# A state-space scan inside a convolution, attention and expert kernel: tiles of 32 channels by 4 states instead of 8 channels by 16 states

## The reference, cut to what matters

```
# 4 directions k (rows, columns, and both reversed), D = 192 channels, N = 16 states, L = 1024 positions
x_dbl = einsum('bkdl,kcd->bkcl', xs, x_proj_weight)      # c = 6 + 16 + 16
dts, B, C = x_dbl[:, :, :6], x_dbl[:, :, 6:22], x_dbl[:, :, 22:38]
dt = softplus(einsum('bkrl,kdr->bkdl', dts, dt_projs_weight) + bias)
A  = -exp(A_logs)                                        # one value per direction, channel and state
for l in range(L):                                       # for every image, direction, channel d, state n
    h[d, n] = h[d, n] * exp(dt[d, l] * A[d, n]) + dt[d, l] * u[d, l] * B[n, l]
    y[d, l] = sum over n of h[d, n] * C[n, l]
y += Ds * u ; the four directions are summed, normalised, passed through gelu
```

## Time and profile before

| | |
|---|---|
| median of 3 runs | 3044.75 us (3038.03 to 3046.68) |
| the profiled execution | 3046.35 us, span 3044.2 us |
| DVE busy over the span | 2226.7 us (73%) |
| PE busy | 2434.6 us (80%) |
| ACT busy | 1408.0 us (46%) |
| POOL busy | 1310.4 us (43%) |
| DMA, mean over the span | 96 GB/s |

### The profile page before, as it was taken

One profiled execution on the slowest core, in us unless ns is written; L12 is line 12 of the kernel. 1 busy time (PEld: TensorE's weight loads), 2 busy tenths in 40 slices (PEclk: granted clock), 3 DMA queues, 4 the chain that ended last, 5 costly groups with the idle time before them and its releaser, 6 DMA issues. The chain is left out here.

```text
span 3044.2 us, 33683 instructions
## 1 busy us (share of the span) xinstructions
PE 2434.6 (80%) x9156; PEld 870.9 (29%) x9156; DVE 2226.7 (73%) x3030; ACT 1408.0 (46%) x1949; POOL 1310.4 (43%) x677
## 2 busy tenths in 40 slices
PE   4776767676677676767667689999999969999999
PEld 2111111111111111111113312323233216676676
DVE  4899989999999998999965588878787843221122
ACT  3344444444444454444545416767676732212221
POOL 1678877878778887778772200000000020000000
PEclk9776767777777776777767869999999969999999
DMA  3455555555555555555541431312213160000000
GB/s 90 131 166 161 157 155 155 171 157 153 158 162 150 164 171 146 158 151 159 161 114 49 105 44 23 43 24 34 34 23 43 23 144 1 11 6 6 6 6 11
DMA packets 104457, 291.18 MB, mean 96 GB/s; under 512 B 15262, under 2 KB 21057, under 8 KB 104257
## 3 DMA queue, kind: packets, MB, share of 16 engines
q1 hardware_dynamic: 103194, 289.13, 36.5%
q10 hardware_dynamic: 1102, 0.19, 0.0%
HBM read 239.66 MB, written 25.88 MB: 87 GB/s over the span
## 5 line engine op out<-in xcount | busy, mean ns | idle before, releaser
L529 POOL TENSOR_TENSOR hs<-hs,bc 128x1024 f32<-128x1024 f32 x384 | 899.9, 2355 | 218.8 <-DVE hs L615 218.6
L502 ACT ACTIVATE decay<-decay,a_neg 128x1024 f32<-128x1024 f32 x384 | 440.6, 1148 | 670.4 <-DMA decay<-dt_rows 659.3
L426 PE MATMUL psU<-stack,spread_sel 96*128 96x512 bf16 x768 | 361.4, 488 | 437.4 <-DVE hs L615 341.8
L1447 DVE TENSOR_REDUCE mx<-ps 128x1 f32<-128x512 f32 x864 | 539.5, 684 | 115.3 <-PE ps L1286 110.2
L559 DVE TENSOR_TENSOR psU<-psU,bc 128x512 f32<-128x512 f32 x768 | 517.3, 677 | 27.1 <-issue 14.9
L1422 ACT ACTIVATE P<-ps 128x512 f32<-128x512 f32 x768 | 417.7, 599 | 247.1 <-PE ps L1298 222.9
L615 DVE TENSOR_TENSOR_SCAN hs<-decay,psU 128x512 f32<-128x512 f32 x384 | 466.2, 1214 | 77.3 <-PE psY L388 49.0
L615 DVE TENSOR_TENSOR_SCAN hs<-decay,hs,psU 128x512 f32<-128x512 f32 x384 | 488.9, 1273 | 1.1
L388 PE MATMUL psY<-hs,state_sel 128*32 128x512 f32 x1572 | 398.5, 849 | 23.7 <-DVE Y L572 11.1
L1286 PE MATMUL ps<-ks,qs 96*128 96x512 bf16 x864 | 344.3, 402 | 34.5 <-DMA ks<-qk_parts 23.8
L426 PEld LDWEIGHTS psU<-stack,spread_sel 96*128 96x128 bf16 x768 | 70.8, 100 | 1005.9 <-DVE hs L615 806.4
(11 more groups left out here) (239 smaller groups left out, 2381.2 us busy)
## 6 DMA issues: line engine op xcount, KB each, us to landing
decay<-dt_rows SPq DMA_DIRECT2D x388, 512.0 KB
stack<-parts SPq DMA_DIRECT2D x297, 64.0 KB, 5.6
dt_rows<-dt SPq DMA_DIRECT2D x33, 384.0 KB, 6.9
qs<-qk_parts SPq DMA_DIRECT2D x90, 128.0 KB, 6.7
ks<-qk_parts SPq DMA_DIRECT2D x90, 128.0 KB, 7.1
qk_parts<-qparts SPq DMA_DIRECT2D x16, 576.0 KB, 3.6
X<-in_x_dram SPq DMA_DIRECT2D x4, 768.0 KB, 9.9
raw<-in_x_dram SPq DMA_DIRECT2D x4, 768.0 KB, 10.5
```

Of the source, the lines that this page charges most:

```text
L426: pe.matmul(psU[:, q % UR, :], s.spread_sel[:, gg, :], stack[:, ui % 2, j, CH * pos:CH * pos + CH], start=True, stop=True).then_inc(dtu_sp ...
L502: nc.scalar.activation(decay[:, t % DR, :], decay[:, t % DR, :], ACT.Exp, scale=s.a_neg[:, col:col + 1]).then_inc(decay_ready, 1)
L529: pool.tensor_tensor(h, h, bc[:, 2 * p + r, 1, :], ALU.mult).then_inc(hc_ready, 1)
L1447: v.reduce_max(mx[:, slot, u:u + 1], ps1[:, (slot * MAXES + u) % R, :], AX.X).then_inc(max_done, 1)
```

## The change

A tile now holds 32 channels x 4 states: partition 32*q + d is channel d, state group q, and tile t = 3*nq + j covers channels 32*j to 32*j+31 and states nq, 4+nq, 8+nq and 12+nq. What has to be spread over the partitions changes with it:

- dt comes from DRAM once for each block of 32 channels (three loads in a unit, into a ring of four `dt_rep`), and serves four tiles. ACT reads `dt_rep` and writes `decay`, which now has six buffers.
- dt*u is stored to DRAM as well and loaded in the same way (three loads, ring `dtu_rep`). DVE's product reads it.
- B is projected together with C by one narrow matmul group (64 rows, both reversals) twice in an image, split into three bf16 parts in `b_stack`, and spread by PE (`b_sel`).
- C goes to DRAM as 32 rows and is loaded four times in a unit, 4 rows each repeated 32 times (`c_rep`). POOL reads it.
- The weights' prologue copies get smaller, the A table comes in its new layout by four DMAs instead of one and a transpose, and z is prepared one unit ahead instead of two, at tiles 1 to 3.

```diff
-        HR, DR, UR = 6, 4, 4
+        HR, DR, UR, RR = 6, 6, 4, 4
-        bc = sb("bc", [128, 4, 2, L])
-        stack = sb("stack", [HC, 2, NBLK, L], BF16)
+        rows = sb("rows_bc", [3 * 2 * N, L])
+        b_stack = sb("b_stack", [3 * 2 * N, 2, L], BF16)
+        c_rep = sb("c_rep", [128, SUB, L])
+        dt_rep = sb("dt_rep", [128, RR, L])
+        dtu_rep = sb("dtu_rep", [128, RR, L])
...
+        def rep_slot(ui, j):
+            return (3 * ui + j) % RR
...
 # PE
-                        pe.wait_ge(stacked[ui % 2], in_stack(b, ui))
+                        if ui in (0, 4):
+                            pe.wait_ge(lo_ready, b * 2 + (p + 1))
...
-                                pe.matmul(psU[:, q % UR, :], s.spread_sel[:, gg, :],
-                                          stack[:, ui % 2, j, CH * pos:CH * pos + CH],
+                                pe.matmul(psU[:, q % UR, :], s.b_sel[:, r, nq, :],
+                                          b_stack[:, p, CH * pos:CH * pos + CH],
...
 # ACT
-                            act.wait_ge(landed[t % DR], n * (16 * TILES // DR) + (16 * (t // DR) + 16))
-                            nc.scalar.activation(decay[:, t % DR, :], decay[:, t % DR, :], ACT.Exp,
+                            if nq == 0:
+                                act.wait_ge(dt_in[rep_slot(ui, j)], rep_count(b, ui, j))
+                            act.wait_ge(scan_done, n * (2 * TILES) + (2 * t + 2 - 2 * DR + S0))
+                            nc.scalar.activation(decay[:, t % DR, :], dt_rep[:, rep_slot(ui, j), :], ACT.Exp,
...
 # POOL
+                            if t % NBLK == 0:
+                                pool.wait_ge(c_in[nq], n * 16 + 16)
...
-                            if t == 2:
-                                pool.wait_ge(hi_ready, n + 2)
-                                pool.tensor_tensor(rest[:], dtu[:], parts[:, 0, :], ALU.subtract).then_inc(rest_ready, 1)
-                            if t == 9:
-                                pool.wait_ge(log_ready, n + 3)
+                            if t == 3:
+                                pool.wait_ge(log_ready, n + 2)
                                 pool.tensor_tensor(dt[:], dt[:], soft[:], ALU.add).then_inc(dt_ready, 1)
...
 # DVE
+                    if t < NBLK and q % 2 == 0:
+                        v.wait_ge(dtu_in[rep_slot(ui, j)], rep_count(b, ui, j))
...
-                    v.tensor_tensor(u, u, bc[:, 2 * p + r, 0, CH * pos:CH * pos + CH], ALU.mult).then_inc(dbu_ready, 1)
+                    v.tensor_tensor(u, u, dtu_rep[:, rep_slot(ui, j), CH * pos:CH * pos + CH], ALU.mult
+                                    ).then_inc(dbu_ready, 1)
...
 # SP
-                    src = s.dt_dram[par, d:d + DD, :].unsqueeze(1).broadcast_to([DD, N, L])
-                    sp.dma_start(decay[:, t % DR, :], src).then_inc(landed[t % DR], 16)
+                def spread_rows(i, par, rep, landed, ui, j):
+                    src = s.dt_dram[par, i, BLK * j:BLK * j + BLK, :].unsqueeze(0).broadcast_to([4, BLK, L])
+                    sp.dma_start(rep[:, rep_slot(ui, j), :], src).then_inc(landed[rep_slot(ui, j)], 16)
...
+                def load_c(ui, nq):
+                    p, f, r, k = order(ui)
+                    src = s.c_dram[p].rearrange("(r q n) l -> r n q l", r=2, q=4)[r, nq]
+                    sp.dma_start(c_rep[:, nq, :], src.unsqueeze(1).broadcast_to([4, BLK, L])).then_inc(c_in[nq], 16)
...
                         sp.wait_ge(dt_ready, n + 2)
+                        store(0, par, dt, dt_stored)
...
+                        c_free(0)
+                        load_c(nu, 0)
+                        sp.wait_ge(dtu_ready, n + 2)
+                        store(1, par, soft, dtu_stored)
+                        sp.wait_ge(dt_stored, n * 16 + 32)
+                        sp.wait_ge(decay_ready, n * TILES + 1)
+                        load_dt(nu, 0)
+                        c_free(1)
+                        load_c(nu, 1)
...
+                        for j in (1, 2):
+                            sp.wait_ge(decay_ready, n * TILES + (9 + j))
+                            load_dt(nu, j)
+                        sp.wait_ge(dtu_stored, n * 16 + 32)
+                        sp.wait_ge(dbu_ready, n * (2 * TILES) + 2)
+                        load_dtu(nu, 0)
+                        sp.wait_ge(dbu_ready, n * (2 * TILES) + 20)
+                        load_dtu(nu, 1)
+                        c_free(2)
+                        load_c(nu, 2)
+                        sp.wait_ge(dbu_ready, n * (2 * TILES) + 22)
+                        load_dtu(nu, 2)
+                        c_free(3)
+                        load_c(nu, 3)
```

More of the change, by code:

```diff
@@ L256, in _ @@
                         q = 2 * k + f
[L257 to L260, removed]
+                        own(v.tensor_copy(s.w_bc[:, k % 2, f, :].rearrange("p (i r n) -> p r i n", i=2, n=N)[:, k // 2],
+                                          ps[0:HC, 1, 38 * q + R:38 * q + R + 2 * N].rearrange("p (i n) -> p i n", n=N)))
                 v.wait_ge(aexp, 1)
@@ L292, in scan @@
         psP = ctx.enter_context(nc.psum_tensor("psP", [128, 2, CH], F32))
-        landed = [sem(f"landed{i}") for i in range(DR)]
+        B_ROWS, C_ROWS, R_ROWS = slice(0, 2 * N), slice(2 * N, 4 * N), slice(4 * N, 6 * N)
+        dt_in = [sem(f"dt_in{i}") for i in range(RR)]
+        dtu_in = [sem(f"dtu_in{i}") for i in range(RR)]
+        c_in = [sem(f"c_in{i}") for i in range(SUB)]
         decay_ready = sem("decay_ready")
-        dtu_spread = sem("dtu_spread")
+        b_spread = sem("b_spread")
         dbu_ready = sem("dbu_ready")
@@ L493, in _ @@
-                for t in (9, 10, 11):
-                    z_side(t, 1, 1)
+                row_mid(0, 0)
+                z_side(3, 0, 0)
                 with act.Fori(0, NB, 1) as b:
@@ L621, in _, with store @@
             def _(sp):
-                def store(par):
-                    sp.dma_start(s.dt_dram[par], dt[:]).then_inc(dt_stored, 16)
-                def stack_up(part, slot):
-                    for j in range(NBLK):
-                        sp.dma_start(stack[BLK * part:BLK * part + BLK, slot, j, :],
-                                     parts[BLK * j:BLK * j + BLK, part, :]).then_inc(stacked[slot], 16)
-                def load(par, t):
-                    d = rows_of(t)
-                    src = s.dt_dram[par, d:d + DD, :].unsqueeze(1).broadcast_to([DD, N, L])
-                    sp.dma_start(decay[:, t % DR, :], src).then_inc(landed[t % DR], 16)
+                def store(i, par, tile, done):
+                    sp.dma_start(s.dt_dram[par, i], tile[:]).then_inc(done, 16)
@@ L635, in _, with store_c @@
+                def store_c(p):
+                    sp.dma_start(s.c_dram[p], rows[C_ROWS, :]).then_inc(c_stored, 16)
+                sp.wait_ge(row_taken, 2)
+                store_c(0)
                 sp.wait_ge(dt_ready, 1)
-                store(0)
+                store(0, 0, dt, dt_stored)
+                sp.wait_ge(dtu_ready, 1)
+                store(1, 0, soft, dtu_stored)
                 sp.wait_ge(dt_stored, 16)
-                for t in range(DR):
-                    load(0, t)
@@ L640, in _ @@
-                for part, ready in enumerate((hi_ready, mid_ready, lo_ready)):
-                    sp.wait_ge(ready, 1)
-                    stack_up(part, 0)
+                load_dt(0, 0)
+                sp.wait_ge(dtu_stored, 16)
+                load_dtu(0, 0)
+                for j in (1, 2):
+                    load_dt(0, j)
+                    load_dtu(0, j)
+                sp.wait_ge(c_stored, 16)
+                for nq in range(SUB):
+                    load_c(0, nq)
                 with sp.Fori(0, NB, 1) as b:
@@ L661, in _ @@
-                for i in range(DR):
-                    sp.wait_ge(landed[i], NB * UNITS * (16 * TILES // DR) + 16)
-                sp.wait_ge(stacked[0], (NB * UNITS // 2 + 1) * (16 * QPART * NBLK))
+                        store(0, par, dt, dt_stored)
+                        if nu in (0, 4):
+                            sp.wait_ge(c_stored, b * 32 + (32 if nu else 48))
+                            sp.sem_inc(turn_seen, 1)
+                        c_free(0)
+                        load_c(nu, 0)
@@ new lines, in _ @@
+                        load_c(nu, 2)
[3 more added lines that the diff above has]
+                        load_c(nu, 3)
+                for j in range(NBLK):
+                    slot = rep_slot(0, j)
+                    sp.wait_ge(dt_in[slot], rep_count(NB, 0, j))
+                    sp.wait_ge(dtu_in[slot], rep_count(NB, 0, j))
+                for nq in range(SUB):
+                    sp.wait_ge(c_in[nq], (NB * UNITS + 1) * 16)
```

327 lines of the change are left out of this document (166 added, 161 removed).

## The result

| | before | after |
|---|---|---|
| median | 3044.58 us (3038.03 to 3046.68, 4 runs) | 3682.16 us (3674.00 to 3684.12, 4 runs) |
| ratio | | 1.209 (95%: 1.207 to 1.212) |
| span of the profiled execution | 3044.2 us | 3681.9 us |
| DMA, mean over the span | 96 GB/s | 69 GB/s |

The changed kernel is 21% slower. It does not lose by more work: the page of after has PE, DVE, ACT and POOL all a little less busy in microseconds than before, and DVE's share has fallen from 73% to 60%.

What follows compares the result with a forecast made beforehand. It took the scan to be bound by loads on four engines: 96.9 us for the first unit, 31 periods of 82.85 and a last load put the next stage at 2774; 3046.35 + 2774 - 1558.4 gave 4260 us, range 3570 to 4530.

Steps and rivals of the forecast that it cites:

- the main case: Scan loads on four engines at the mean or low rate: 4260 us, range 3900 to 4520, chance 0.62.
- the upper rate: Rival for the scan's loads: four engines at 26.4 GB/s each, 5.0 us a load, 3604 us (3550 to 3800), chance 0.24.
- The outermost count sets the engines: Scan loads: the source's outermost count sets how many engines run, 8 before and 4 after, always the same ones.
- The rate of one engine: Scan loads: 18.3 GB/s an engine, so 7.2 us for a 512 KB load; bounds 5.0 and 8.0 us.
- The cycle of a unit: Scan: DVE and POOL work, two stores, then nine loads in a row make a period of 82.85 us, against 46.0.
- 18.05 + 9 L: Scan: a unit's period in us, 18.05 for compute and stores plus nine loads of L us each.
- τ: Scan: the moment when a unit's last load of dt*u (`dtu_rep`, j = 2) has landed.
- Start and end: Around the scan's periods: dt store at 52.8 us, next stage at 2774; A table's four small loads 0 to 12 us.
- 621 + 299 L: End of the scan: the time in us when the next stage starts, with L us for one load.
- The reading of before: Scan before the change: bound by its loads on eight engines almost as tightly as by DVE; ACT waited 659.3 us.
- Engines by distinct rows: Rival for the scan's loads: distinct source rows set the engines, only C gets four; 52 us a unit, 3240 us, chance 0.05.
- The case of more engines: Rival: loads spread over 8 to 16 engines, DVE and PE decide the scan; 2988 us, chance 0.05.

Runs made afterwards that it cites:

- the run of before on all engines: Kernel before with states outermost in a tile (partition 8*n + d), so each decay load's source is 16 copies of 8 rows: 3009.87 us, ratio 0.989.
- the kernel made for it: Changed kernel with the partition order turned over, 4*d + q instead of 32*q + d, channel outermost: 2971.12 us, ratio 0.976 to before.

## Why the prediction was right or wrong

It gave 4260 us, 3570 to 4530, slower with 0.94; the time is 3682. The direction and the mechanism were right, and one term was mis-sized, by enough that the change came out at 638 us where 1215 were forecast. The 3900 to 4520 given for the main case alone missed; 3570 to 4530 holds the result because the upper rate, a rival with a chance of 0.24, was kept in it.

- *The outermost count sets the engines.* Right. The share in loads is 0.26, and the three layouts and the split transfers agree: 4, 8 or 16 engines by that count, in the old tiles and in the new. This was seen ahead of the run in the earlier trace rows, where X with 96 rows outermost had 1.04 and `decay` with 8 had 0.51. The rule of the Trainium skill (DMA: Bandwidth & Descriptors, "Rules for kernel authors"), that a leading broadcast of c copies confines a DMA to c engines, is what after shows for c = 4, with 102 to 104 GB/s.
- *The rate of one engine.* The step that failed. The prediction took "the mean of the whole scan, 7.2 us" (18.3 GB/s an engine) for one load and gave the upper rate a chance of 0.24. Measured: 102/4 = 25.5 to 104/4 = 26.0 GB/s, 5.1 us, and 4.92 us at the end of the scan. The mean over eight engines was an average of fast and slow stretches, and its slow part doesn't carry over to four. It was carried over without a row that showed it, as the prediction says itself. Nothing in before told the two rates apart either: 62 to 66 us, with four loads queued, ran at 127 GB/s. The sign that the prediction named for this error, a share of 0.25 with 100 GB/s or more, is what the windows show.
- *The cycle of a unit.* Right. With L = 5.1 the formula 18.05 + 9 L gives 63.95 us; 65.05 were measured. The addition on POOL ends at 1023.24, 13.6 us after τ (13.4 predicted), and the store is issued at once. The share of 0.26 to the end of a burst of loads says that the waits between them were met in time. In the unit shown, of 65.5 us, 0.2 of the excess lies before the store of dt and 1.3 behind it; why was not looked into.
- *Start and end.* The first store of dt at 55.57 against 52.8 predicted, the first scan at 74.7. The next stage at 2187 us, by 621 + 299 L at 5.1 it is 2146. Of the 41 us some 34 are 31 periods that are 1.1 longer, and 3 the later store. The four small loads of the A table, allowed 0 to 12 us, cost little: with one DMA in their place, in the kernel with the channel outermost, the store is issued at 54.60, 1 us earlier.
- *The sum.* The own formula at the measured L gives 3046.35 + 2146 - 1558.4 = 3634 us, within 1.3% of 3682. The rival *four engines at their upper rate* (3604 us, 3550 to 3800) is what came.
- *The reading of before.* Right in kind, too strong in degree. "Almost as tightly as by DVE" comes to 34 us of 3044, by the run of before on all engines, and ACT's 659.3 us of waits were mostly no cost.
- *The other rivals.* Engines by distinct rows fell with the share of 0.26 in loads of 32 distinct rows. The case of more engines was worked out at 2988 us; the kernel made for it took 2971, with the wait at the place that was named.

What stays open: why eight engines move now 127 and now 211 GB/s at a standing share, and why a busy one of 16 moves now 14 and now 26. The pitch of the rows was tried and changes little if anything, and the number of rows is not it. The half loads on four engines write the same partitions of the same tiles and held 105 GB/s in the window shown, 26 an engine, so that neither the destination nor the source rows alone explain it. How many engines run at once, and with how many loads in flight, would be the next things to vary; that was not tried.

## What to carry to other kernels

When a tile repeats rows over partitions, look at the outermost count of each load's source and choose the order of the indices in a partition number so that it is 16 or a multiple (here 16, 32 and 96 used all engines). In this kernel one exchange of two indices is worth 711 us of 3682. A DMA share that stands at 4/16 or 8/16 while consumers wait is a full resource, not a free one. But idle time of a consumer that is ahead, as ACT's here, doesn't price it. For the rate that a changed resource will run at, don't carry a mean over from a stage whose stretches differ: give the time for both ends, and run the new pattern in the old kernel. The loads of before cut in two are an edit of a few lines and would have shown 105 GB/s on four engines ahead of the forecast.

## What was not expected of the hardware

The rate of a busy engine isn't one number, and it is steadiest where few engines run. Four engines stand at 102 to 105 GB/s (26 each) in the mid-scan windows of two different kernels; in after's first loads, 62 to 66 us, they moved 85. Eight run anywhere from 127 to 211 (16 to 26 each) at a share of 0.51 to 0.52. Sixteen reach 416 in the best stretch shown (26 each), but 264 at a share of 0.88 (18.8 each) in the same kernel and 201 at 0.89 (14.1 each) in the old tiles. So with more engines the total rises, and the rate of each one can't be counted on. Loads cut into four transfers of 32 partitions moved 16.0 GB/s per busy engine where whole ones, with the channel outermost, moved 20.5, without a cost to the time that one run could tell.
